# Output-projection weights from the third pair of heads on loaded from GpSimd's own queue, each behind the low part that frees its place

## The chip, the cores and the metric

One core of one Trainium2 chip runs the kernel. The metric is device time in microseconds (us) of one launch. The kernel before took 1513.62 us, the median of three runs (1512.69 to 1514.01). A change is called faster, the same or slower here with a bound of 0.2%, that is 3.0 us.

## What is computed

A gated cross-attention block on x (4 batches, 512 rows, 1024 columns) with a context of 64 rows a batch, then a feed-forward part, all in float32. Cut to what matters:

```python
x = x + tanh(g_xattn) * attention(layernorm(x), ctx, ctx, mask, wq, wk, wv, wo)
x = x + tanh(g_ffn) * ffn(layernorm(x), weight, bias, gate_w, in_scale, out_scale)

# attention: 32 query heads, 8 key heads, 128 wide, rotary positions
attn = softmax(q @ k.T / sqrt(128) + mask)
out  = (attn @ v).reshape(bs, sq, 32 * 128) @ wo          # wo: 4096 x 1024
# ffn: signs of the weight, scales from a softmax routing over 8 experts
out  = ((x * (routing @ in_scale)) @ sign(weight).T) * (routing @ out_scale) + bias
```

## The kernel before, in words

Every large product is made of float32r parts: a matrix is cast to a high part (`hi`), the rest (`raw - hi`) is its low part (`lo`), and three matmuls (hi by hi, lo by hi, hi by lo) stand for one (`three`, lines 51 to 53). ScalarE casts the high parts, GpSimd subtracts for the low parts of the weights.

The program has four stages. **Preparation** (to about 90 us): keys, values, normalised and turned x. **Heads** (90 to 880 us): queries, scores and softmax of 16 pairs of heads; the probabilities go to a scratch tensor in HBM. **Phases** (880 to 1300 us): eight phases, each one batch by one half of the 1024 output columns. A phase runs over the 16 pairs of heads (`HP`): `probs_times(phase, hp)` adds probabilities by (values by output weights) into four PSUM banks. The products of values and output weights, `values_wo(k, h)`, are made once for two batches; k counts 64 pairs of heads over four rounds (`ROUNDS * HP`), and a round is a long phase, with its `values_wo`, and a short one that uses what was kept. In phase 0 `values_wo` runs two pairs ahead of `probs_times`, in the other long phases three. **Feed-forward** (from 1300 us): blocks of 256 rows.

The output weights are what the change touches. `wo_raw` has two places (`WO_BUFS = 2`) of 512 KB, place k % 2. Pair k passes through these steps:

1. `load_wo(k)` (line 695): SyncE waits until the low parts of pair k - 2 are done, and issues one DMA of 512 KB (line 698). Its semaphore is `wo_in[k % 2]`.
2. `split_wo(k, h)` (ScalarE, line 1120): two casts w_hi<-w_raw, each behind the load.
3. `split_low(k, h)` (GpSimd, line 1363): two subtractions w_lo<-w_raw,w_hi, each behind its cast. The second frees the place for pair k + 2.
4. `values_wo(k, h)` (TensorE), then `split_vw` (ScalarE, lines 1128 and 1131) and `values_low` (VectorE, lines 1502 and 1505) take its result out of PSUM; `probs_times` waits for these.

The order of each engine is written out by hand. SyncE issues nearly all transfers in one in-order queue: the loads of output weights, the stores and loads of probabilities (lines 677 and 688), x in and x1 out (lines 728 and 733). At which pair of a phase it comes to which `load_wo` stood in three tables, of which one reads

```python
LONG_WO = {0: 7, 1: 8, 2: 9, 3: 10, 4: 11, 5: 12, 6: 13, 7: 14, 8: 15, 9: 16, 11: 17, 12: 18, 13: 19}
```

(at pair hp of a long phase, `load_wo` of pair 16 * round + value). Probabilities are replaced four pairs behind TensorE (`P_LAG`). ScalarE casts pair hp + 5 at pair hp of a long phase (hp + 3 in phase 0), GpSimd runs through all 64 pairs in order, and does the last steps of the softmax between pairs 3 and 8 (`turned_low`, line 1304, `over_sums`, line 1310). In the heads stage GpSimd's order is that of `step` (line 1312 on).

## Time and profile before

| | |
|---|---|
| median of three runs | 1513.62 us |
| the profiled execution | 1511.08 us, its span 1509.3 us |
| mean granted TensorE clock | 0.994 |
| busy: TensorE, weight loads | 1459.8 us (97%), 1205.7 us (80%) |
| busy: VectorE, ScalarE, GpSimd | 990.7 us (66%), 568.8 us (38%), 718.8 us (48%) |
| DMA queues | SyncE's and ScalarE's only carry the large loads: 213.30 MB in q1, 43.9% of 16 engines' span |
| loads of output weights | 64 of 512 KB, 5.0 us median from issue to landing |

A duration in the profile is that of one instruction; matmuls overlap, so that of a row of them the starts tell the pace. "Idle before" is the time for which an engine stood still ahead of an instruction, and behind the arrow stands what ended that. SPq is SyncE's queue: its rows are the issuing of transfers, not the transfers.

### The profile page before, as it was taken

Reading aid. Unit: us, or ns where it says so; the run is one execution under the profiler, and the core shown is the slowest. Engines: PE = TensorE matmul, PEld = TensorE weight load, DVE = VectorE, ACT = ScalarE, POOL = GpSimd, SP = SyncE. Lnnn points to the kernel's source line nnn. Section 1 sums busy time; section 2 is a strip of 40 time slices with the busy share of each in tenths; the row PEclk is TensorE's granted clock in tenths of the full one; section 3 lists DMA queues with packets and bytes.
Section 4 is the critical chain, followed back from the end, with each engine's and each line's share of the span. In section 5 each row is a group of like instructions: output and inputs, shape, how many; then the busy total and the mean of one; then the engine's idle time right before and its main releaser. Section 6 shows DMA issues by size and latency. Waiting matters only on the chain.

```text
span 1509.3 us, 21232 instructions
## 1 busy us (share of the span) xinstructions
PE 1459.8 (97%) x6800; PEld 1205.7 (80%) x6800; DVE 990.7 (66%) x2117; ACT 568.8 (38%) x927; POOL 718.8 (48%) x594
## 2 busy tenths in 40 slices
PE   6989999999999999999999978999999999999998
PEld 5878888888888888888888856887887887878887
DVE  5837788888888887788888885436346246535653
ACT  5732222222222222222222266438348347124542
POOL 5744455554655546545555465325226235025554
PEclk9999999999999999999999999999999999999999
DMA  7830222122221222122211497889989979742321
GB/s 271 292 116 15 80 82 70 50 68 69 76 69 42 76 69 69 56 76 76 69 61 52 102 310 232 271 271 295 328 300 297 338 271 304 259 168 84 112 75 65
DMA packets 105441, 225.99 MB, mean 150 GB/s; under 512 B 11104, under 2 KB 21856, under 8 KB 105248
## 3 DMA queue, kind: packets, MB, share of 16 engines
q1 hardware_dynamic: 99184, 213.30, 43.9%
q10 hardware_dynamic: 6192, 11.86, 2.1%
q8 instruction: 36, 0.59, 0.2%
q14 instruction: 29, 0.24, 0.1%
HBM read 167.45 MB, written 57.67 MB: 149 GB/s over the span
## 4 chain that ended last, share of the span: by engine, by line
PE 84%; issue 3%; POOL 2%; DMA 2%; SPq 1%; DVE 1%; ACT 1%; POOLq 0%; ACTq 0%; DVEq 0%
PE bank L51 19%; PE bank L53 18%; PE bank L52 18%; PE bank L903 7%; PE bank L904 7%; PE bank L905 7%; PE bank L927 5%; DMA w_raw<-in_wo 1%; POOL last_rows L1358 1%; SPq L688 1%; PE bank L942 1%; POOL feed L1350 0%; POOL w_lo L1363 0%; PE bank L951 0%; PE bank L974 0%
## 5 line engine op out<-in xcount | busy, mean ns | idle before, releaser
L51 PE MATMUL bank<-x_hi,w_hi 128*128 128x512 f32 x1024 | 399.9, 391 | 3.9 <-PEq L66 3.9
L52 PE MATMUL bank<-x_lo,w_hi 128*128 128x512 f32 x1024 | 399.6, 390 | 0.0
L53 PE MATMUL bank<-x_hi,w_lo 128*128 128x512 f32 x1024 | 399.6, 390 | 0.0
L1363 POOL TENSOR_TENSOR w_lo<-w_raw,w_hi 128x512 fp32r<-128x512 f32 x128 | 162.4, 1291 | 235.6 <-ACT w_hi L1120 235.6
L1297 POOL TENSOR_TENSOR q_lo<-rot,q_hi 128x512 fp32r<-128x512 f32 x128 | 164.9, 1294 | 185.6 <-ACT q_hi L1061 185.4
L51 PEld LDWEIGHTS bank<-x_hi,w_hi 128*128 128x128 f32 x1024 | 192.9, 188 | 44.2 <-issue 4.1
L52 PEld LDWEIGHTS bank<-x_lo,w_hi 128*128 128x128 f32 x1024 | 193.0, 188 | 40.1
L53 PEld LDWEIGHTS bank<-x_hi,w_lo 128*128 128x128 f32 x1024 | 192.9, 188 | 40.1
L1061 ACT CAST q_hi<-rot 128x512 fp32r<-128x512 f32 x128 | 79.6, 622 | 344.2 <-DVE rot L1423 290.7
L1502 DVE TENSOR_TENSOR project<-bank,project 64x512 fp32r<-64x512 f32 x128 | 87.4, 683 | 166.7 <-ACT project L1128 164.7
L1304 POOL TENSOR_TENSOR pt_lo<-pt,pt_hi 128x512 fp32r<-128x512 f32 x64 | 82.4, 1288 | 144.4 <-ACT pt_hi L1071 144.3
L1418 DVE TENSOR_TENSOR bank<-bank,cos_q 128x512 f32<-128x512 f32 x64 | 44.8, 699 | 136.5 <-PE bank L53 136.5
L927 PE MATMUL bank<-feed,feed 128*128 128x512 f32 x512 | 130.3, 399 | 0.0
L903 PE MATMUL bank<-project,project 128*128 128x512 f32 x320 | 125.4, 392 | 0.0
L905 PE MATMUL bank<-project,project 128*128 128x512 f32 x320 | 124.7, 390 | 0.0
L904 PE MATMUL bank<-project,project 128*128 128x512 f32 x320 | 124.6, 389 | 0.0
L1128 ACT CAST project<-bank 64x512 fp32r<-64x512 f32 x128 | 74.2, 579 | 113.5 <-PE bank L53 111.1
L927 PEld LDWEIGHTS bank<-feed,feed 128*128 128x128 f32 x512 | 95.1, 190 | 21.8 <-issue 2.9
L1065 ACT ACTIVATE shifted<-shifted 128x512 f32<-128x512 f32 x64 | 40.5, 633 | 166.8 <-DVE shifted L1449 166.8
L1505 DVE TENSOR_TENSOR project<-bank,project 64x512 fp32r<-64x512 f32 x128 | 88.8, 694 | 4.0
L1291 POOL TENSOR_TENSOR w_lo<-w_raw,w_hi 128x1024 fp32r<-128x1024 f32 x30 | 72.2, 2406 | 37.6 <-ACT w_hi L1054 37.6
L1120 ACT CAST w_hi<-w_raw 128x512 fp32r<-128x512 f32 x128 | 73.1, 618 | 40.4 <-DMA w_raw<-in_wo 37.5
(141 smaller groups left out, 2632.3 us busy)
## 6 DMA issues: line engine op xcount, KB each, us to landing
project<-probs_scratch SPq DMA_DIRECT2D x160, 256.0 KB, 6.3
w_raw<-in_wo SPq DMA_DIRECT2D x64, 512.0 KB, 5.0
p_left<-probs_scratch SPq DMA_DIRECT2D x96, 256.0 KB, 6.6
w_raw<-in_wq SPq DMA_DIRECT2D x32, 512.0 KB, 5.2
probs_scratch<-pt_hi SPq DMA_DIRECT2D x64, 256.0 KB, 2.6
probs_scratch<-pt_lo SPq DMA_DIRECT2D x64, 256.0 KB, 3.2
x_in<-in_x SPq DMA_DIRECT2D x16, 512.0 KB, 5.4
last_rows<-in_x SPq DMA_DIRECT2D x8, 1024.0 KB, 9.2
```

Source lines behind the costliest of these rows:

```text
L51: pe.matmul(out, hi, rhs_hi, start=first, stop=False, **kw)
L52: pe.matmul(out, hi, rhs_lo, start=False, stop=False, **kw)
L53: return pe.matmul(out, lo, rhs_hi, start=False, stop=last, **kw)
L903: pe.matmul(acc_ps[t][:], p_hi[hp][:, at], vw, start=hp == 0, stop=False)
L904: pe.matmul(acc_ps[t][:], p_hi[hp][:, at], vw_low, start=False, stop=False)
L905: last = pe.matmul(acc_ps[t][:], p_lo[hp][:, at], vw, start=False, stop=hp == HP - 1)
L927: last = pe.matmul(f_ps[c % 2][:], part[j][k // 4][:, k % 4, t * P:(t + 1) * P], w_sign[k][:, h * HW:(h + 1) * HW], start=(k == 0 and n == ...
L1297: nc.gpsimd.tensor_tensor(q_lo[:, c], rot[:, c], q_hi[:, c].bitcast(F32), ALU.subtract).then_inc(q_lo_ready, 1)
L1304: nc.gpsimd.tensor_tensor(pt_lo[:, i], pt[:], pt_hi[:, i].bitcast(F32), ALU.subtract).then_inc(pt_lo_ready, 1)
L1363: nc.gpsimd.tensor_tensor(wo_lo[:, i, h], wo_raw[:, i, h], wo_hi[:, i, h].bitcast(F32), ALU.subtract).then_inc(wo_lo_ready, 1)
L1502: nc.vector.tensor_tensor(vw_first_lo[k % VW_BUFS][rows_of], vw_bank(k, h)[0:SK, :], vw_first_hi[k % VW_BUFS][rows_of].bitcast(F32), ALU.s ...
L1505: nc.vector.tensor_tensor(vw_kept_lo[hp][rows_of], vw_bank(k, h)[SK:P, :], vw_kept_hi[hp][rows_of].bitcast(F32), ALU.subtract).then_inc(vw ...
```

## The change

`load_wo` loses its wait and stays on SyncE for pairs 0 and 1 alone. The 62 others are issued by GpSimd, by a new function `next_wo(k)` that stands in its program right behind the second low part of pair k, waits until that is complete, and issues the load of pair k + 2 into the same place. These loads have semaphores of their own (`wo_next`), for which ScalarE's casts wait. The three tables and all their calls on SyncE go.

```diff
-    FIRST_WO = {5: 11, 6: 12, 7: 13, 8: 14, 9: 15, 11: 16, 12: 17, 14: 18, 15: 19}
...
+        wo_next = [sem(f"wo_next{i}") for i in range(WO_BUFS)]
...
             def load_wo(k):
 
-                wait(sp, wo_lo_ready, 2 * (k - WO_BUFS) + 2)
                 sp.dma_start(wo_raw[:, k % WO_BUFS], a["wo"][k // HP % NH, k % HP]).then_inc(wo_in[k % WO_BUFS], 16)
...
-            load_wo(2)
-            load_wo(3)
             sp.wait_ge(masked_ready, HEAD_STEPS)
             first_probs(10)
-            load_wo(4)
...
                 for hp in range(HP):
-                    if hp in upcoming and rnd * HP + upcoming[hp] < ROUNDS * HP:
-                        load_wo(rnd * HP + upcoming[hp])
                     due = place(phase, hp) - P_LAG
...
-                act.wait_ge(wo_in[k % WO_BUFS], 16 * (k // WO_BUFS + 1))
+                if k < WO_BUFS:
+                    act.wait_ge(wo_in[k], 16)
+                else:
+                    act.wait_ge(wo_next[k % WO_BUFS], 16 * (k // WO_BUFS))
...
+            def next_wo(k):
+
+                if k + WO_BUFS < ROUNDS * HP:
+                    pool.wait_ge(wo_lo_ready, 2 * k + 2)
+                    nxt = k + WO_BUFS
+                    pool.dma_start(wo_raw[:, k % WO_BUFS], a["wo"][nxt // HP % NH, nxt % HP]).then_inc(wo_next[k % WO_BUFS], 16)
+
             over_key_heads(pool, step)
+            next_wo(0)
             split_low(1, 0)
             query_low(LAST_G, STEPS_G - 1)
             split_low(1, 1)
+            next_wo(1)
             for k in range(2, ROUNDS * HP):
                 for h in range(2):
                     split_low(k, h)
+                next_wo(k)
                 if k == 3:
                     turned_low(LAST_G, 5)
                     over_sums(LAST_G, 6)
```

SyncE's queue before, at the end of the softmax and the beginning of phase 0 (w_raw<-in_wo at L698 are the loads of pairs 9 and 10, then 11, then 12; project and p_left are places of the probabilities; last_rows is the place of x):

```order
L698 DMA w_raw<-in_wo 128x1024 [waits wo_lo_ready] x2
L677 DMA probs_scratch<-pt_hi 128x512 [waits pt_lo_ready,pt_hi_ready]
L677 DMA probs_scratch<-pt_lo 128x512
L780 DMA gate_x<-in_g_xattn 128x1 [waits pt_stored1,pt_stored0]
L781 DMA gate_f<-in_g_ffn 128x1
L728 DMA last_rows<-in_x 128x4x512
L688 DMA project_0_6<-probs_scratch 128x512 [waits av_done]
L688 DMA project_1_6<-probs_scratch 128x512
L698 DMA w_raw<-in_wo 128x1024 [waits wo_lo_ready]
```

The same place of SyncE's queue now:

```order
L675 DMA probs_scratch<-pt_hi 128x512 [waits pt_lo_ready,pt_hi_ready]
L675 DMA probs_scratch<-pt_lo 128x512
L768 DMA gate_x<-in_g_xattn 128x1 [waits pt_stored1,pt_stored0]
L769 DMA gate_f<-in_g_ffn 128x1
L725 DMA last_rows<-in_x 128x4x512
L686 DMA project_0_6<-probs_scratch 128x512 [waits av_done]
L686 DMA project_1_6<-probs_scratch 128x512
```

The load of pair 11 no longer stands behind the wait for the stored probabilities, x and two loads of probabilities. GpSimd before, from the low parts of pairs 4 to 6 on:

```order
L1363 TENSOR_TENSOR w_lo<-w_raw,w_hi 128x512 [waits wo_hi_ready] x6
L1304 TENSOR_TENSOR pt_lo<-pt,pt_hi 128x512 [waits pt_stored0,pt_hi_ready]
L1310 TENSOR_TENSOR probs<-shifted,row_inv 128x512 [waits pt_ready,inv_ready]
L1363 TENSOR_TENSOR w_lo<-w_raw,w_hi 128x512 [waits wo_hi_ready] x4
L1304 TENSOR_TENSOR pt_lo<-pt,pt_hi 128x512 [waits pt_stored1,pt_hi_ready]
L1363 TENSOR_TENSOR w_lo<-w_raw,w_hi 128x512 [waits wo_hi_ready] x48
```

GpSimd now, from the low parts of pair 6 on (L1350 are the low parts, L1357 the loads of pairs 8, 9, 10 and 11):

```order
L1350 TENSOR_TENSOR w_lo<-w_raw,w_hi 128x512 [waits wo_hi_ready] x2
L1357 DMA w_raw<-in_wo 128x1024 [waits wo_lo_ready]
L1291 TENSOR_TENSOR pt_lo<-pt,pt_hi 128x512 [waits pt_stored0,pt_hi_ready]
L1297 TENSOR_TENSOR probs<-shifted,row_inv 128x512 [waits pt_ready,inv_ready]
L1350 TENSOR_TENSOR w_lo<-w_raw,w_hi 128x512 [waits wo_hi_ready] x2
L1357 DMA w_raw<-in_wo 128x1024 [waits wo_lo_ready]
L1350 TENSOR_TENSOR w_lo<-w_raw,w_hi 128x512 [waits wo_hi_ready] x2
L1357 DMA w_raw<-in_wo 128x1024 [waits wo_lo_ready]
L1291 TENSOR_TENSOR pt_lo<-pt,pt_hi 128x512 [waits pt_stored1,pt_hi_ready]
L1350 TENSOR_TENSOR w_lo<-w_raw,w_hi 128x512 [waits wo_hi_ready] x2
L1357 DMA w_raw<-in_wo 128x1024 [waits wo_lo_ready]
```

The issue of a load stands between two pairs of low parts, and ahead of GpSimd's last steps of the softmax.

## Rows read from the trace of the kernel before

**Rows 1.** The page: engines, and TensorE in 40 equal slices of the span

```profile
PE 1459.8 (97%) x6800; PEld 1205.7 (80%) x6800; DVE 990.7 (66%) x2117; ACT 568.8 (38%) x927; POOL 718.8 (48%) x594
PE   6989999999999999999999978999999999999998
```

**Rows 2.** Busy time by stretch: start:end, length, then engines, granted clock, DMA share, GB/s

```profile
878.00:888.00 10.00, 7.48 (x25) 5.14 (x24) 8.27 (x16) 5.22 (x9) 5.44 (x5) 0.83 0.95 330
...
928.00:938.00 10.00, 5.62 (x24) 4.05 (x22) 3.12 (x5) 4.50 (x8) 2.84 (x3) 1.00 0.90 316
938.00:948.00 10.00, 9.87 (x37) 8.04 (x38) 5.50 (x8) 7.01 (x13) 5.48 (x5) 0.83 0.85 276
```

**Rows 3.** TensorE in order of time: start, duration, instruction [idle before <-what ended it]

```profile
887.72 0.47 PE L51 MATMUL bank<-w_hi,project 128*128 128x512 f32 x1 [0.90 <-ACT w_hi L1120]
888.98 0.47 PE L51 MATMUL bank<-w_hi,project 128*128 128x512 f32 x1 [0.33 <-POOL w_lo L1363]
...
928.22 0.39 PE L905 MATMUL bank<-project,project 128*128 128x512 f32 x1
...
932.30 0.39 PE L905 MATMUL bank<-project,project 128*128 128x512 f32 x1
936.70 0.47 PE L51 MATMUL bank<-w_hi,project 128*128 128x512 f32 x1 [4.01 <-DVE project L1505]
...
1265.71 0.47 PE L51 MATMUL bank<-w_hi,vt_left 128*128 128x512 f32 x1 [1.88 <-ACT w_hi L1120]
```

**Rows 4.** The chain that ended last, around the longest of these waits

```profile
919.72 4.06 DMA probs_scratch<-pt_lo
...
924.70 0.43 SPq L728
925.18 0.50 SPq L688
...
926.20 7.15 DMA w_raw<-in_wo
```

**Rows 5.** SyncE's queue in order of time: issues only

```profile
875.52 7.56 SPq L698 DMA_DIRECT2D w_raw<-in_wo  x2
...
1252.92 0.56 SPq L728 DMA_DIRECT2D last_rows<-in_x  x1
1256.01 0.33 SPq L698 DMA_DIRECT2D w_raw<-in_wo  x1
```

**Rows 6.** GpSimd in order of time

```profile
868.06 2.54 POOL L1363 TENSOR_TENSOR w_lo<-w_raw,w_hi 128x512 fp32r<-128x512 f32 x2 [0.17 <-ACT w_hi L1120]
872.34 1.05 POOL L1310 TENSOR_TENSOR probs<-shifted,row_inv 128x512 f32<-128x512 f32 x1
876.21 1.27 POOL L1363 TENSOR_TENSOR w_lo<-w_raw,w_hi 128x512 fp32r<-128x512 f32 x1 [2.82 <-ACT w_hi L1120]
...
912.98 5.03 POOL L1363 TENSOR_TENSOR w_lo<-w_raw,w_hi 128x512 fp32r<-128x512 f32 x4
...
920.85 2.55 POOL L1363 TENSOR_TENSOR w_lo<-w_raw,w_hi 128x512 fp32r<-128x512 f32 x2 [1.59 <-ACT w_hi L1120]
```

**Rows 7.** ScalarE in order of time: casts that waited for a load

```profile
885.65 1.14 ACT L1120 CAST w_hi<-w_raw 128x512 fp32r<-128x512 f32 x2 [3.81 <-DMA w_raw<-in_wo]
...
933.37 1.14 ACT L1120 CAST w_hi<-w_raw 128x512 fp32r<-128x512 f32 x2 [6.07 <-DMA w_raw<-in_wo]
```

**Rows 8.** Line 698: issue to landing, of the 5 loads from 1150 to 1170 us

```profile
DMA to landing us min/median/max: 3.4/4.3/7.3
```

**Rows 9.** GpSimd's shortest instruction, by form: busy us, mean ns of one

```profile
L1381 POOL MEMSET ffn_minus_one<- 128x2 f32 x1 | 0.1, 100 | 0.0
```

**Rows 10.** The page: low parts of the output weights, and of the heads' weights

```profile
L1363 POOL TENSOR_TENSOR w_lo<-w_raw,w_hi 128x512 fp32r<-128x512 f32 x128 | 162.4, 1291 | 235.6 <-ACT w_hi L1120 235.6
...
L1291 POOL TENSOR_TENSOR w_lo<-w_raw,w_hi 128x1024 fp32r<-128x1024 f32 x30 | 72.2, 2406 | 37.6 <-ACT w_hi L1054 37.6
```

**Rows 11.** SyncE's queue: what it waited for from 850 to 1300 us (us, times, longest)

```profile
SPq L698 <- POOL w_lo L1363: 195.3, 57, 8.7
```

More of the change, by code:

```diff
@@ L344, in attend_and_finish @@
     SHORT_VW = {4: 0, 8: 1, 12: 2}
-    FIRST_WO = {5: 11, 6: 12, 7: 13, 8: 14, 9: 15, 11: 16, 12: 17, 14: 18, 15: 19}
-    LONG_WO = {0: 7, 1: 8, 2: 9, 3: 10, 4: 11, 5: 12, 6: 13, 7: 14, 8: 15, 9: 16, 11: 17, 12: 18, 13: 19}
-    SHORT_WO = {4: 20, 8: 21, 12: 22}
     P_LAG = 4
@@ L757, in _ @@
             over_key_heads(sp, step)
-            load_wo(2)
-            load_wo(3)
             sp.wait_ge(masked_ready, HEAD_STEPS)
             first_probs(10)
-            load_wo(4)
             first_probs(11)
-            load_wo(5)
             store_probs(LAST_G, 5)
             first_probs(12)
-            load_wo(6)
             first_probs(13)
-            load_wo(7)
             first_probs(14)
-            load_wo(8)
             store_probs(LAST_G, 6)
             first_probs(15)
-            load_wo(9)
-            load_wo(10)
             store_probs(LAST_G, 7)
@@ L784, in _ @@
             for phase in range(PHASES):
-                rnd, long = phase // PB, phase % PB == 0
-                upcoming = SHORT_WO if not long else FIRST_WO if rnd == 0 else LONG_WO
                 for hp in range(HP):
-                    if hp in upcoming and rnd * HP + upcoming[hp] < ROUNDS * HP:
-                        load_wo(rnd * HP + upcoming[hp])
                     due = place(phase, hp) - P_LAG
```

## The prediction

> **What bounds the kernel now.** I read the page first. TensorE is busy for 97% of the span, and its slices are full but for the beginning and one place, the 24th and 25th slice, with the digits 7 and 8 [rows 1]. A slice is 37.7 us, so that place is 868 to 943 us: the end of the heads and the start of phase 0. Everything that the change touches lies from there to 1300 us. The granted clock and the busy time by stretch come next: of the 10 us from 928 on TensorE works 5.62, and in the 10 us behind that the mean granted clock is 0.83; from 878 on both happen together [rows 2]. In the order of time on TensorE I then looked for idle times and for what ended them. Those that lead back to a load of output weights are few: 0.90 and 0.33 us before pair 2, 4.01 us before the instruction at 936.70, and 1.88 us at 1265.71 in the last long phase [rows 3]. The other waits of the stretch, each 0.3 to 2.1 us, end on the last steps of the softmax, and the change leaves them.
>
> The chain that ended last tells how the 4.01 us came about [rows 4]. SyncE first waits until the last low part of the probabilities is stored (919.72 and 4.06 us), then issues the two gates, x (1 MB) and two loads of probabilities (256 KB each), and only then, at 926.20, the load of pair 11, which takes 7.15 us to land. ScalarE had stood still for 6.07 us by then [rows 7]. The place of this load had been free since 920.85 + 2.55 = 923.40 us, when GpSimd ended the low parts of pair 9 [rows 6]. So 2.8 us are lost before the issue, and more behind it, since the load stands behind 1.5 MB in the same queue: loads that found less ahead of them landed in 3.4 us at best and 4.3 in the median [rows 8].
>
> **Two places make a loop.** Low parts of pair k end, the load of pair k + 2 is issued, lands, its first half is cast (0.6 us, half of the 1.14 in [rows 7]), two low parts take 2.54 us [rows 6], and the place is free again. With the median landing that is 0.6 + 2.54 + 4.3 = 7.4 us for two pairs. TensorE needs 18 matmuls for a pair: 4.08 us from 928.22 to 932.30 [rows 3], 8.2 us for two. The loop has 0.8 us to spare where nothing delays a load.
>
> **What the change takes away.** SyncE spent 195.3 us of its queue in waiting for low parts, in 57 waits [rows 11]. That is no time of TensorE: where SyncE had been waiting before the low part ended, the load was issued at once. The gain is where it came late or had traffic ahead.
>
> *Pair 11.* Pair 9's low parts depend on what GpSimd does between. From 912.98 on it works on pairs 7 and 8 for 5.03 us without a break [rows 6]; two issues now stand in it, so the last low part of the probabilities ends some 2 us later and pair 9's about 0.5 us later, at 923.9. With the issue the load is on its way at 925, about when x is, from another queue. I take 5 us for landing, between 4.3 and 7.15, counted from the start of the issue: 929 us instead of 933.35. TensorE resumed 3.35 us behind the landing (936.70 - 933.35), so now at 932.4 to 933, and it was free at 932.7. Of 4.01 us some 0.6 are left: 3.4 saved. The stretch behind had a clock of 0.83, 1.7 us lost in 10, which I expect back, since the two stretches with such a drop in [rows 2] are the ones in or just behind which TensorE was busy for 7.5 and 5.6 of 10 us. **Together -5.1 us.**
>
> *Pair 2.* The place is free at 868.06 + 2.54 = 870.6 us, SyncE issues at 875.52 [rows 5], behind 20 loads of probabilities, and ScalarE waits 3.81 us, until 885.65 [rows 7]. Now GpSimd issues behind its row at 872.34 [rows 6], at 873.4, in idle time, since it then waited until 876.21 [rows 6]. The load is 2 us earlier and shares the engines with the backlog instead of standing behind it. The 0.90 and 0.33 us [rows 3] should go: **-1.2 us**. The pause ahead of them, and its slow clock, stays.
>
> *The last long phase.* The load issued at 1256.01 stood behind x, issued at 1252.92 [rows 5], and 1.88 us of TensorE followed [rows 3]. From its own queue it should land 1 to 2 us earlier, less a later issue: **-0.9 us**.
>
> **What it adds.** GpSimd issues 62 loads and waits before each until its own low part is complete. No row shows an issue on GpSimd. The bounds are its shortest instruction, 0.10 us, and its longest, 2.41 us [rows 9, 10]. I take 1.05 us, that of the row at 872.34, one pass of GpSimd over 128 partitions and the middle of the range [rows 6]. Nothing speaks for less than none. The same load took SyncE 0.33 us [rows 5], so the loop grows by 0.7 us, to 8.1, against 8.2. With the median it still fits; with a load of 5 us it does not, by 0.6. In the long phases from the second round on ScalarE works two pairs ahead of TensorE (8.2 us), which covers that. In phase 0 the lead is smaller, and of its pairs behind 938 us I charge three turns at 0.3 us: **+1.0 us**. Between 893 and 925 the loop is not what ends the waits. GpSimd's 62 issues in sum, 65 us, fit into the 235.6 us in which it waited for casts [rows 10]. SyncE's queue moves ahead: loads of probabilities go as soon as TensorE has used the old ones, some pairs earlier than before. TensorE waited for none of them before, so that gives nothing; x and x1 go earlier too, but for the first x, 2 us later and not wanted before phase 0 ends. The feed-forward part is as it was.
>
> **Sum**, against the profiled execution of 1511.1 us: -5.1 - 1.2 - 0.9 + 1.0 = -6.2, so 1504.9. Its runs' median lies 2.5 us above that execution: 1507.4 us, 0.4% less.
>
> **A rule against this.** In the rows, the load of pair 11 took 7.15 us and others in a thinner stretch 3.4 to 4.3 [rows 4, 8]; I read the difference as the 1.5 MB ahead of it in the queue. The Trainium skill, DMA: Bandwidth & Descriptors, section "Issuing engines are not separate DMA queues", says that transfers from all engines interleave on the same 16 DMA engines, and that a second issuing engine saves only the time of the issue. The same page, "Queues, rings and completion order", says that each of these engines takes turns between queues, packet by packet; by that a load on its own queue would pass a backlog. No row before shows two loaded queues side by side in this stretch.
>
> **The rivals.**
> 1. *Only the issue moves.* The 7.15 us are the price of the traffic, whichever queue the load is in. Then pair 11 starts at 925 less about 0.3 instead of 926.20 and TensorE's wait shrinks by 1.5 us; a pause of 2.5 remains, the clock may or may not drop. Pair 2 gives 0.5, the last phase nothing, the loop costs 1.0: -1.0 to -2, 1512 us, not to be told from no change. By the first of the two rules of the Trainium skill (DMA: Bandwidth & Descriptors) it would be this one. For it: the DMA engines' share is 0.90 from 928 to 938 us [rows 2]. Against it: loads of the same size landed in half the time. Chance 0.22.
> 2. *GpSimd becomes the bound (slower).* If an issue holds GpSimd, or delays the landing, by x us more than SyncE's did, the loop is 7.4 + x against 8.2. With x = 2.1 (its longest instruction) it lacks 1.3 us for two pairs: 8 turns of phase 0, 10 us; three long phases of 6.5 turns, 8.5 us each less the lead of 8.2, 1 us; and GpSimd's last steps of the softmax come late. +11 to +14 less the 6 of gains: 1520 us. It decides from about 8 (x - 0.8) = 7, x = 1.7. For it: nothing shows the price of an issue. Against: GpSimd waits 235.6 us for casts [rows 10]. Chance 0.15.
> 3. *More than the one load.* All loads from 883 to 925 land nearer 3.4 than 5 us, ScalarE never stands, and half of the small waits of phase 0 go as well, another 3 to 4 us: 1503.5 us. Chance 0.13.
>
> That the loads aren't moved at all is excluded by the order. The forecast has 0.50.
>
> **How the numbers follow.** The forecast's own range is 1504 to 1510, from an issue of 0.10 to 1.3 us and a landing of 4.3 to 6 us. With the third rival and the first it reaches from 1503 to 1513, and part of the second brings it to 1517; what lies outside is the dear half of the second, and a gain beyond the third. Faster by over 0.2% (3.0 us, what a measurement of this kernel can tell from no change): 0.50 + 0.13 = 0.63. Within it: 0.22. Slower: 0.15.
>
> **What would show it.** In the profile after: an issue on GpSimd's queue of about 1 us, 62 times; SyncE's waits for low parts gone; no wait of TensorE over 1.5 us from 889 to 1300 us; ScalarE's wait of 6.07 us at most 2; the clock at 1.00 from 928 to 948; loads of output weights at 4 to 5 us in the median. Issues of more than 1.7 us, or waits of TensorE for casts spread over all long phases, would prove the forecast wrong towards slower. A pause of over 2 us left in front of pair 11's or 12's products with a landing of 7 us would be the first rival.

## The result and the profile after

| kernel | median us | runs | lowest to highest | profiled execution | span |
|---|---|---|---|---|---|
| before | 1513.82 | 4 | 1512.69 to 1514.33 | 1511.08 | 1509.3 |
| after | 1525.45 | 4 | 1523.72 to 1525.68 | 1525.49 | 1523.7 |

The ratio is 1.0075, interval 1.0058 to 1.0093: **slower**, where I had forecast 0.4% less. By the medians the change costs 11.6 us. The profiled execution is 14.4 us longer, because that of before lies 2.7 us below the median of its runs; every table of phases below is read from one profile for each kernel. The page of after, against [rows 1] and [rows 10]:

```profile
span 1523.7 us, 21232 instructions
PE 1464.0 (96%) x6800; PEld 1204.3 (79%) x6800; DVE 990.7 (65%) x2117; ACT 568.2 (37%) x927; POOL 754.4 (50%) x656
PE   5889999999999999999999978999999999999998
L1350 POOL TENSOR_TENSOR w_lo<-w_raw,w_hi 128x512 fp32r<-128x512 f32 x128 | 162.3, 1283 | 194.9 <-ACT w_hi L1107 194.8
w_raw<-in_wo POOLq DMA_DIRECT2D x62, 512.0 KB, 6.1
```

Nothing in the busy times tells where the time went: GpSimd has 62 more instructions and 36 us more, and TensorE is busy for 96%. The one number that speaks is the last: a load of output weights takes 6.1 us in the median to land; on the page of before it took 5.0.

The view that answers is that of the windows, one for each phase. TensorE does the same 272 matmuls in each of the three long phases that follow phase 0. First after, then before; the columns are the length, the busy time of TensorE, of its weight loads, of VectorE, ScalarE and GpSimd, the granted clock, the DMA share and GB/s.

```profile
1012.14:1078.24 66.10, 63.45 (x272) 50.01 (x271) 38.51 (x56) 45.05 (x78) 39.98 (x40) 1.00 0.83 258
1125.85:1191.70 65.85, 63.77 (x272) 51.55 (x271) 38.51 (x57) 46.02 (x79) 39.86 (x38) 0.97 0.83 261
1239.30:1304.60 65.30, 63.69 (x272) 49.91 (x271) 41.45 (x64) 45.16 (x76) 34.18 (x34) 1.00 0.80 249
```

```profile
1008.08:1070.70 62.62, 61.82 (x272) 50.47 (x271) 38.52 (x56) 45.06 (x78) 33.12 (x28) 1.00 0.88 284
1118.30:1180.69 62.39, 61.74 (x272) 50.53 (x271) 38.53 (x56) 46.06 (x79) 33.05 (x26) 1.00 0.88 285
1228.29:1293.18 64.89, 62.26 (x272) 50.38 (x271) 41.45 (x63) 45.17 (x76) 29.02 (x25) 1.00 0.86 287
```

Each window runs from one end of a phase to the next; an end is the start of VectorE's four instructions that add the last products of a phase to x. In the first two long phases all is the same work, 3.5 us longer. In the second of them the clock has a part in it: by its mean of 0.97 it stood for a short time at the lower of its two levels (1.2 GHz instead of 2.4), which takes 1.7 of the 65.85 us, and before has 1.00 there. TensorE's idle time, the length less its busy time, is 2.65 us in the first of them instead of 0.80. GpSimd's busy time grows by 6.9 us, its 12 issues. The DMA share falls from 0.88 to 0.83: the same bytes in a longer time. What changed is when they are carried, and beside what. The 14.4 us, by the same marks:

| part | before | after | difference |
|---|---|---|---|
| until GpSimd's first low part of output weights | 868.06 | 869.23 | +1.2 |
| from there to the end of phase 0 | 92.46 | 95.32 | +2.9 |
| long phases 2, 4, 6 | 62.62, 62.39, 64.89 | 66.10, 65.85, 65.30 | +3.5, +3.5, +0.4 |
| short phases and the feed-forward part | | | +0.1 |
| from the end of GpSimd's last addition to the end of the span | 2.52 | 5.39 | +2.9 |

The first line lies ahead of the change; over all the profiles below that moment lies between 865.4 and 870.3, so it is chance. The last long phase is 64.9 us here and up to 67.9 in other profiles with all loads on SyncE and the same order in that phase (z1_early), so nothing is read from it alone. The same holds for small differences in phase 0: the mean granted clock over it is 0.96 in before and 0.94 in x3_one, whose code is the same up to the last long phase, and that alone is 1.7 us.

**The start of phase 0.** TensorE, then ScalarE and GpSimd, in order of time, beside [rows 3, 7, 6]:

```profile
894.93 0.47 PE L51 MATMUL bank<-w_hi,project 128*128 128x512 f32 x1 [2.18 <-DVE project L1502]
...
927.72 0.47 PE L51 MATMUL bank<-w_hi,project 128*128 128x512 f32 x1 [0.51 <-ACT w_hi L1107]
...
942.04 0.49 PE L51 MATMUL bank<-w_hi,project 128*128 128x512 f32 x1 [2.48 <-POOL w_lo L1350]
```

```profile
930.60 1.14 ACT L1107 CAST w_hi<-w_raw 128x512 fp32r<-128x512 f32 x2 [0.49 <-DMA w_raw<-in_wo]
...
938.72 1.14 ACT L1107 CAST w_hi<-w_raw 128x512 fp32r<-128x512 f32 x2 [4.20 <-DMA w_raw<-in_wo]
```

```profile
893.26 0.57 POOL L1357 DMA_DIRECT2D w_raw<-in_wo  x1 [0.30 <-POOL w_lo L1350]
893.85 1.28 POOL L1291 TENSOR_TENSOR pt_lo<-pt,pt_hi 128x512 fp32r<-128x512 f32 x1
...
926.83 0.57 POOL L1357 DMA_DIRECT2D w_raw<-in_wo  x1 [0.30 <-POOL w_lo L1350]
927.42 2.54 POOL L1350 TENSOR_TENSOR w_lo<-w_raw,w_hi 128x512 fp32r<-128x512 f32 x2
930.25 0.57 POOL L1357 DMA_DIRECT2D w_raw<-in_wo  x1 [0.30 <-POOL w_lo L1350]
```

Pair 11, whose load landed in 3.7 us, is as forecast: ScalarE waits 0.49 us for it, not 6.07. The next one, pair 12, is issued at 930.25 and lands 8.4 us later; ScalarE waits 4.20 us, TensorE 2.48. That load was no quicker before. The load of pair 12 in before, issued at 927.78:

```profile
DMA to landing us min/median/max: 8.5/8.5/8.5
```

TensorE's pause ahead of pair 11 had hidden it. What is new are the loads behind it: those of pairs 13 to 16 took 3.5 to 4.4 us before and take 6.6 to 8.8 now. SyncE's queue tells what lay beside them:

```profile
928.76 0.43 SPq L725 DMA_DIRECT2D last_rows<-in_x  x1
929.24 14.15 SPq L686 DMA_DIRECT2D project<-probs_scratch  x20
```

x and twenty loads of probabilities in 14 us. No low part held SyncE back any more, so the queue let go at once what before had gone out two and four at a time, each time behind a load of weights. The windows, against [rows 2]:

```profile
888.00:898.00 10.00, 6.78 (x28) 4.77 (x27) 7.82 (x17) 7.45 (x14) 7.48 (x8) 1.00 0.85 254
928.00:938.00 10.00, 10.00 (x45) 8.26 (x44) 5.50 (x8) 5.49 (x10) 5.65 (x6) 1.00 0.91 286
938.00:948.00 10.00, 7.42 (x25) 5.26 (x25) 5.51 (x8) 6.91 (x12) 6.15 (x6) 0.83 1.03 384
948.00:958.00 10.00, 9.13 (x39) 6.94 (x39) 5.42 (x8) 7.13 (x14) 6.21 (x6) 1.00 1.05 391
```

The ten microseconds that TensorE had lost are full, and the two windows behind are not: DMA share over 1.0, and again a mean granted clock of 0.83. The 2.18 us at 894.93 are the other new wait. At first it looks like the price of an issue: GpSimd's low part of the probabilities starts at 893.85, directly behind an issue, and before it started at 891.32, or 1.4 us earlier when the 1.2 us ahead of the change are taken off. But x4_act (below), where GpSimd issues nothing, has the same wait:

```profile
894.86 0.77 PE L51 MATMUL bank<-w_hi,project 128*128 128x512 f32 x1 [2.23 <-DVE project L1510]
```

and x2_tiny, where GpSimd issues and the loads stay on SyncE, has 0.77 us there, near the 0.58 of before. So the wait came with the loads' other queue, not with GpSimd's issue. In both kernels that have it ScalarE first stood still for the load of pair 3 (2.68 us in after, 2.57 in x4_act), which landed at 889.7 in after and at 887.0 before (1.2 us of the difference lie ahead of the change).

**A long phase.** SyncE's queue in the first of them, after, and then before:

```profile
1019.88 0.38 SPq L725 DMA_DIRECT2D last_rows<-in_x  x1
1020.31 39.18 SPq L686 DMA_DIRECT2D project<-probs_scratch  x20
```

```profile
1020.50 0.33 SPq L698 DMA_DIRECT2D w_raw<-in_wo  x1
1020.88 0.90 SPq L688 DMA_DIRECT2D p_left<-probs_scratch  x2
...
1028.65 0.33 SPq L698 DMA_DIRECT2D w_raw<-in_wo  x1
1029.03 1.61 SPq L688 DMA_DIRECT2D p_left<-probs_scratch  x2
1030.69 0.59 SPq L728 DMA_DIRECT2D last_rows<-in_x  x1
```

Before, one load of weights went out, and right behind it two of probabilities: the weights had the start on what followed. Now the probabilities go when TensorE frees their places, and x goes 7.7 us into the phase instead of 22.6. From 1012 to 1078 us a load of weights lands in 4.4, 6.0 and 8.0 us (least, median, most); those of before in 3.6, 4.7 and 7.8. The waits of 850 to 1310 us:

```profile
ACT w_hi L1107 <- DMA w_raw<-in_wo: 55.5, 34, 4.4
POOL w_raw L1357 <- POOL w_lo L1350: 18.1, 61, 0.3
```

ScalarE waits for 34 loads and 55.5 us, where before it was 20 and 37.5.

### The profile page after: what moved, and what is told of

It is laid out like the page before. It is cut to its first block, busy times and chain, and to the rows that moved or that the text cites. A ratio compares the mean times of both kernels' runs of the same rounds, so it can differ in the third digit from the quotient of the medians.

```text
span 1523.7 us, 21232 instructions
## 1 busy us (share of the span) xinstructions
PE 1464.0 (96%) x6800; PEld 1204.3 (79%) x6800; DVE 990.7 (65%) x2117; ACT 568.2 (37%) x927; POOL 754.4 (50%) x656
## 4 chain that ended last, share of the span: by engine, by line
PE 82%; POOL 4%; DMA 3%; issue 3%; DVE 1%; ACT 1%; POOLq 0%; ACTq 0%; DVEq 0%; SPq 0%
PE bank L51 19%; PE bank L52 19%; PE bank L53 19%; PE bank L887 7%; PE bank L889 7%; PE bank L888 7%; PE bank L911 5%; DMA w_raw<-in_wo 3%; POOL w_lo L1350 2%; POOL last_rows L1345 1%; PE bank L926 1%; POOL feed L1337 0%; PE bank L935 0%; PE bank L958 0%; PE bank L903 0%
## 5 line engine op out<-in xcount | busy, mean ns | idle before, releaser
L1350 POOL TENSOR_TENSOR w_lo<-w_raw,w_hi 128x512 fp32r<-128x512 f32 x128 | 162.3, 1283 | 194.9 <-ACT w_hi L1107 194.8
L1107 ACT CAST w_hi<-w_raw 128x512 fp32r<-128x512 f32 x128 | 73.2, 618 | 58.2 <-DMA w_raw<-in_wo 55.5
L1502 DVE TENSOR_TENSOR project<-bank,project 64x512 fp32r<-64x512 f32 x128 | 88.8, 694 | 4.0
```

Of the source, the lines that this page charges most:

```text
L1350: nc.gpsimd.tensor_tensor(wo_lo[:, i, h], wo_raw[:, i, h], wo_hi[:, i, h].bitcast(F32), ALU.subtract).then_inc(wo_lo_ready, 1)
L1502: nc.vector.tensor_tensor(vw_kept_lo[hp][rows_of], vw_bank(k, h)[SK:P, :], vw_kept_hi[hp][rows_of].bitcast(F32), ALU.subtract).then_inc(vw ...
```

## The experiments

All ratios are against runs of before on the same chip; the phases are from one profile each, and before's phases are those of the first profile. P0 is the time from GpSimd's first low part of output weights to the end of phase 0, P2, P4 and P6 are the long phases, "tail" is the last line of the table above. "Landing" is the median from issue to landing of the output weights, by the page.

| kernel | ratio [95%] | P0 | P2 | P4 | P6 | tail | landing |
|---|---|---|---|---|---|---|---|
| before | 1 | 92.5 | 62.6 | 62.4 | 64.9 | 2.5 | 5.0 |
| after | 1.0075 [1.0058, 1.0093] | 95.3 | 66.1 | 65.9 | 65.3 | 5.4 | 6.1 |
| x2_tiny | 1.0034 [1.0019, 1.0049] | 94.3 | 63.4 | 64.9 | 65.4 | 5.4 | 4.8 |
| x4_act | 1.0014 [0.9999, 1.0029] | 91.8 | 64.6 | 64.6 | 64.4 | 2.5 | 5.8 |
| x3_one | 1.0028 [1.0015, 1.0041] | 93.0 | 62.8 | 62.5 | 69.0 | 2.5 | 5.0 |
| y1_after_thin | 0.9952 [0.9935, 0.9969] | 89.8 | 61.2 | 61.2 | 61.2 | 5.4 | 3.8 |
| y2_before_thin | 0.9953 [0.9936, 0.9971] | 92.3 | 61.2 | 61.2 | 61.2 | 2.5 | 3.4 |
| x1_paced | 1.0137 [1.0118, 1.0155] | 93.1 | 68.7 | 69.3 | 71.0 | 5.4 | 6.6 |
| u1_landed | 1.0134 [1.0100, 1.0167] | 93.5 | 70.5 | 69.2 | 68.8 | 5.4 | 6.3 |
| v1_behind | 1.0074 [1.0059, 1.0090] | 92.1 | 64.7 | 64.4 | 68.0 | 5.4 | 5.5 |

### What an issue on GpSimd costs: x2_tiny, t8_tiny, t32_tiny

Before, with 62 DMAs that nobody needs (128 rows of 4 bytes) on GpSimd, each where the change has its load and behind the same wait. The other two issue only the first 8 and the first 32.

```
+            def next_tiny(k):
+                if k + WO_BUFS < ROUNDS * HP:
+                    pool.wait_ge(wo_lo_ready, 2 * k + 2)
+                    pool.dma_start(tiny[:, k:k + 1], a["g_xattn"]).then_inc(tiny_in, 16)
```

> The kernel before, and behind each pair of low parts GpSimd also waits and issues a DMA of 128 rows of 4 bytes that nobody needs. Loads of output weights stay on SyncE. Theory 'GpSimd's issue': GpSimd is held 0.9 us a pair, which delays low parts, so +3 to +8 us. Theory 'pacing': under +1.5 us in the phases. Theory 'end': any use of GpSimd's DMA queue adds about 2.9 us behind the last store, which both others have to be read on top of: 1516.7 if the phases cost nothing.

> The kernel before with 8 unneeded DMAs of 128 rows of 4 bytes on GpSimd (62 of them gave 5.4 us from GpSimd's last addition to the end of the span, one load gave 2.48, as in the kernel before). If the end's 2.9 us grow with the number: 2.8 to 2.9 us here. If there is a threshold: 2.5 or 5.4.

> The same with 32. If the end's 2.9 us grow with the number: 3.9 to 4.0 us here. If there is a threshold: 2.5 or 5.4, and with the run above it tells on which side.

An issue keeps GpSimd for 0.56 us, and it waits 0.30 us before it for its own low part. In the profile that goes with 1.9 us more in P0, 0.8, 2.5 and 0.5 in the long phases and 2.9 in the tail: 8.6 us. By the runs it is 0.34%, 5.1 us (2.9 to 7.4), so that 2.3 us (0 to 4.5) are left for the phases instead of 5.7. The windows of P0 and of the second long phase tell why the profile shows more; before, P0 has a mean clock of 0.96 and the long phase 1.00:

```profile
866.47:960.80 94.33, 79.63 (x314) 60.29 (x313) 64.78 (x119) 62.52 (x110) 64.40 (x61) 0.93 0.85 265
1119.40:1184.26 64.86, 63.30 (x272) 51.70 (x271) 38.56 (x57) 46.07 (x79) 40.16 (x39) 0.97 0.89 286
```

The time at 1.2 GHz that these means stand for is worth up to 3.4 us more in P0 and 1.7 in the long phase than before, by the trace's clock; whether the issues brought it is not shown. t32_tiny made 11 issues in the first long phase, where x2_tiny made 13, and it took 62.7 us, as before:

```profile
1010.59:1073.27 62.68, 61.70 (x272) 50.52 (x271) 38.56 (x56) 45.11 (x78) 38.70 (x39) 1.00 0.85 279
```

P0 is longer in all three, 94.1 us with 8 DMAs, 94.8 with 32 and 94.3 with 62, each time with more time at the lower clock than in before. The loads of weights stayed on SyncE and land as before.

**The tail.** It is 2.5 us with 8 DMAs (one run, 1511.51 us), 2.9 with 32 (one run, 1514.62 us), 5.4 with 62. The expectations, growth with the number or a threshold, seem both missed. The trace shows what it is. GpSimd's last instruction but for semaphores is a DRAIN, which starts 1.3 us before its last addition ends. It takes, with 0 (before), 1 (x3_one), 8, 32 and 62 DMAs (after), in nanoseconds, as least, median and most of the one instruction:

```profile
L359 POOLq DRAIN  x1: 1372/1372/1372, 1505.5 to 1505.5; - x1
L359 POOLq DRAIN  x1: 1457/1457/1457, 1507.2 to 1507.2; - x1
L360 POOLq DRAIN  x1: 2038/2038/2038, 1505.9 to 1505.9; - x1
L360 POOLq DRAIN  x1: 3998/3998/3998, 1508.6 to 1508.6; - x1
L356 POOLq DRAIN  x1: 6447/6447/6447, 1517.0 to 1517.0; - x1
```

That is 0.08 us more for every DMA that GpSimd has issued, in proportion, whether of 4-byte rows (x2_tiny has 6448) or of 512 KB. SyncE waits beside it for the last store, until 2.3 us behind the addition, so with 8 DMAs the longer DRAIN is hidden, and with 32 (2.7 us) it begins to show. What the DRAIN does with each of them is not shown.

### Whose queue, and what it shares: x4_act and x3_one

x4_act is the change with the 62 loads issued by ScalarE, each behind the same low part, between its own instructions. x3_one is before with the load of the last pair alone moved to GpSimd.

```
-                    pool.dma_start(wo_raw[:, k % WO_BUFS], ...).then_inc(wo_next[k % WO_BUFS], 16)
+                    act.dma_start(wo_raw[:, k % WO_BUFS], ...).then_inc(wo_next[k % WO_BUFS], 16)
```

> As the change, but the 62 loads are issued by ScalarE behind its copies of the product of the pair before, each behind its low part. A queue of its own for the weights and SyncE freed, but no GpSimd DMA and no software queue. Theory 'pacing': the loads still land in 5.5 to 6.5 us and TensorE still waits in phases 0, 2 and 4: 1518 to 1522. Theory 'GpSimd's issue': with the issue off GpSimd and no cost at the end, 1508 to 1512.

> The kernel before with one load, that of the last pair, issued by GpSimd. Theory 'end' (a fixed cost at the end of a kernel that uses GpSimd's DMA queue at all): +2.5 to +3 us, 1516.5, and 5.4 us instead of 2.5 from the last addition of GpSimd to the end of the span. Its rival, that the 2.9 us at the end come from the 62 loads or by chance: no difference, 1513.8.

With ScalarE as issuer the tail and P0 are those of before or better, but two of the long phases stay 2 us longer, and a load lands in 5.8 us. GpSimd has no DMA in it, so this part comes with the second queue, not with GpSimd. It is not the queue alone: ScalarE now also waits for low parts between its casts. In the profiles the parts nearly add up: x4_act's phases and tail sum to +3.0 us (-0.7, +2.0, +2.2, -0.5), x2_tiny's to 8.6, together 11.6 of the 13.2 us that the change costs from its first line on. By the runs they do so less well: 0.14% and 0.34% are 0.48% of the 0.75%, and the rest is about what the three intervals leave open.

The single load of x3_one, GpSimd's row, SyncE's beside it and TensorE's:

```profile
1273.59 0.73 POOL L1380 DMA_DIRECT2D w_raw<-in_wo  x1 [0.30 <-POOL w_lo L1369]
```

```profile
1270.08 10.79 SPq L689 DMA_DIRECT2D project<-probs_scratch  x14
```

```profile
1284.22 0.61 PE L51 MATMUL bank<-w_hi,vt_left 128*128 128x512 f32 x1 [2.15 <-ACT w_hi L1126]
```

It took 8.6 us to land. The same load on SyncE's queue in before, issued at 1274.09, took 4.0. A wait of 2.15 us of TensorE follows from one load. The 0.28% of the runs, 4.2 us (2.3 to 6.2), is more than that, and so are the 4.1 us of P6. The window from that wait on tells most of the rest:

```profile
1284.00:1294.00 10.00, 9.78 (x36) 7.70 (x37) 5.90 (x11) 6.37 (x9) 2.46 (x5) 0.83 0.63 198
```

Behind the wait a part of it is at 1.2 GHz, another 1.7 us lost, as from 938 on in before. z1_early, which has no DMA on GpSimd, lost 3.0 us in P6 against before, with a wait of 3.6 us instead of 1.9 and a mean clock of 0.97 instead of 1.00. So a long P6 is a late load and what the clock adds, whichever queue the load was in.

### Without the probabilities' traffic: y1_after_thin and y2_before_thin

After and before, each with the reloads of probabilities behind phase 0 cut to 16 of 512 columns. Both leave out most of the probabilities that the later phases read, so their results are wrong and they tell of time alone.

```
-                    sp.dma_start(part[hp].bitcast(F32), scratch["probs"][n, hp, :, batch * S:(batch + 1) * S]).then_inc(p_in[hp], 16)
+                        sp.dma_start(part[hp].bitcast(F32)[:, 0:16], scratch["probs"][n, hp, :, batch * S:batch * S + 16]).then_inc(p_in[hp], 16)
```

> The change, with the loads of probabilities for all phases but the first cut to 16 of 512 columns (the rest is stale, so this leaves out most of the reloaded probabilities); number and order of transfers stay. Theory 'priority' (in SyncE's one queue the weights stood ahead of the probabilities issued behind them; in two queues both share the engines, and a load of weights takes 5.5 to 8 us instead of 4): with nothing to share with, loads of weights land in 3.5 to 4.2 us, phases 2 and 4 fall from 66 to 62 us and under those of the kernel before. Theory 'GpSimd's issue' (0.9 us longer loop, or a slower software queue): loads stay over 5 us, phases 2 and 4 at 65 us. 5.4 us at the end stay with both.

> The kernel before with the same cut loads of probabilities, as the control: it leaves out the same. Both theories: weights land in 3.5 to 4.5 us, phases 2 and 4 at 61.4 to 62.3 us, the wait before pair 11's product in phase 0 about as before or shorter. The difference to the run above, outside of the 2.9 us at the end, is then what GpSimd's issue costs without traffic: 'priority' says under 1 us a long phase, 'GpSimd's issue' 3 us.

The first long phase of y1_after_thin, and the loads by the pages of the two:

```profile
1004.87:1066.07 61.20, 61.20 (x272) 50.67 (x271) 38.56 (x57) 46.15 (x79) 40.64 (x41) 1.00 0.52 162
```

```profile
w_raw<-in_wo POOLq DMA_DIRECT2D x62, 512.0 KB, 3.8
```

```profile
w_raw<-in_wo SPq DMA_DIRECT2D x64, 512.0 KB, 3.4
```

61.20 us is TensorE without a gap, and both kernels reach it in all three long phases, with GpSimd's issues and without. So the issues alone do not make a long phase longer here: they can do it only where a load lands late as well. In P0 y1_after_thin is 2.5 us shorter than y2_before_thin and 5.5 shorter than after: without the traffic the change has a gain there (the pause ahead of pair 11, 4.19 us in y2_before_thin, is gone in it), though y2_before_thin also has more time at the lower clock in P0, which takes up to 3.4 us. The tail takes back 2.9. The two end at the same time, 0.9952 and 0.9953 of before.

### The order of the two queues: x1_paced, u1_landed, v1_behind

The change with SyncE's waits put back where its loads of weights stood, without the loads: until the low parts are done that free the place (x1_paced), until the load has landed (u1_landed), or until GpSimd has issued it, told by a one-column MEMSET behind the issue (v1_behind).

```
+                wait(sp, wo_lo_ready, 2 * (k - WO_BUFS) + 2)
```

```
+                    sp.wait_ge(wo_next[k % WO_BUFS], 16 * (k // WO_BUFS))
```

```
+                    sp.wait_ge(wo_issued, k - WO_BUFS + 1)
```

> The change, with one part undone: SyncE keeps its waits for low parts where its loads of output weights stood, and issues nothing there. GpSimd issues the 62 loads as in the change. Theory 'pacing' (the waits on SyncE spread the loads of probabilities; without them these go in bursts and the weights share the engines with them, 7 to 9 us for a load instead of 4): most of the loss in the phases comes back, loads of weights land in 4.5 to 5 us in the median, time 1514 to 1518. Theory 'GpSimd's issue' (0.3 us of waiting for its own low part and 0.57 us of issue lengthen the loop of two places, and the software queue is slower): the loss stays, 1523 to 1526, landing 6 us.

> The change, but where SyncE's load of output weights stood it now waits until that load, issued by GpSimd, has landed, and only then issues the next loads of probabilities. Theory 'priority': this gives the weights back their place ahead of the probabilities, so they land in 4 to 4.8 us and phases 2 and 4 take 62 to 63.5 us, against 66 in the change and 69 with the waits for low parts. Theory 'GpSimd's issue': the 0.9 us stays in the loop and phases 2 and 4 take 64.5 us or more.

> The change, but SyncE issues its loads of probabilities right behind GpSimd's issue of the load of weights (GpSimd sets one column of a small tensor behind its issue, and SyncE waits for that): the order of issue of the kernel before, in two queues. 'Order of issue counts': weights land in 4 to 4.8 us, phases 2 and 4 take 63 to 64.5 us. 'Two queues share the engines in whatever order, one queue serves the first first': weights land in 5.5 to 6.5 us with the probabilities issued just behind, phases 2 and 4 at 66 to 69 us.

x1_paced missed both of its theories: 1534.5 us, where one gave 1514 to 1518 and the other 1523 to 1526. So it is not the spacing by the waits as such that was lost. In x1_paced the wait that releases SyncE also releases GpSimd, and SyncE is the quicker: the probabilities go out just ahead of the weights each time. The long phases take 69 to 71 us, and from 1012 to 1078 us the loads land in 5.6, 6.9 and 7.8 us; none is quick any more. In v1_behind they go out just behind, and the long phases take 64.7, 64.4 and 68.0 us. Between these two kernels little but the order of issue differs (and a MEMSET of 0.1 us for each load), and it is worth 3.0 to 4.9 us a long phase and 0.6% of the time. Against the change itself v1_behind gains nothing in sum (1.0074 beside 1.0075): 3.3 us less in P0 and 1.4 and 1.5 in P2 and P4, 2.7 more in P6 and 2.2 more in the short phases. That it stays above the 62.5 us of before is partly the price of GpSimd's issues, so how much more an order within one queue is worth cannot be told from it. u1_landed refuted what I had thought: I had expected 62 to 63.5 us from holding the probabilities until the weights are there, and got 69 to 70. My reading is that, held back so long, they meet the next load of weights; it is not tested.

### Repairing the order in one queue: z1_early, z2_late_x, z3_order, z4_x_sooner

If the order is what counts, pair 11's load can be put right without a second queue. All four are before with that load ahead of the wait for the stored probabilities and the first x later in phase 0.

```
             store_probs(LAST_G, 7)
+            load_wo(11)
...
-            load_x(0)
...
+                    if phase == 0 and hp == 8:
+                        load_x(0)
```

z2_late_x moves the later x of the long phases as well, from step 3 to 12. z3_order takes step 8 for them and spreads the loads of phase 0:

```
-    FIRST_WO = {5: 11, 6: 12, 7: 13, 8: 14, 9: 15, 11: 16, 12: 17, 14: 18, 15: 19}
+    FIRST_WO = {5: 12, 6: 13, 7: 14, 8: 15, 9: 16, 11: 17, 13: 18, 15: 19}
...
-                    if phase >= 1 and hp == 3:
+                    if phase >= 1 and hp == (8 if long else 3):
```

z4_x_sooner is z3_order with the first x at step 4.

> The kernel before; on SyncE the load of pair 11 goes ahead of the wait for the stored probabilities, and the first x, which stood ahead of it, goes to pair 8 of phase 0. No GpSimd DMA. My reading of the 4.01 us wait (late issue, and 1.5 MB ahead in the same queue): it goes, with its slow clock, phase 0 shorter by 4 to 5.5 us, time 0.9965 to 0.9975 of before, 1508.5. The rival, that the wait moves to pair 12 or 13: 0.999 to 1.000.

> As z1_early, and in the long phases x is loaded at pair 12 instead of pair 3, behind most loads of weights. Theory 'priority' (what stands ahead of a load of weights in its queue is what delays it): phase 6 falls from 64.9 to 62.5 us, phases 2 and 4 by 0 to 0.5, so another 2 to 3 us less than z1_early. Risk: x comes too late for the end of the phase, then TensorE waits at the start of the next one and a phase grows by some us.

> The kernel before with SyncE's order mended: pair 11 ahead of the wait for the stored probabilities, pairs 12 and 13 one pair of heads earlier, the first x at pair 8 of phase 0, and x in the long phases at pair 8 instead of 12 as in z2_late_x, where it came too late for the end of the phase (67 us). No GpSimd DMA. Theory 'priority': phase 0 shorter by 2 to 4 us, phases 2 and 4 at 62 to 62.5, phase 6 at 63.5: 1507 to 1509, 0.996 to 0.998 of before. If x is still too late, phases 2 and 4 are over 63.

> z3_order with the first x at pair 4 of phase 0 instead of pair 8. If x at pair 8 delays the loads of pairs 15 and 16, which TensorE waited 2.0 us for, phases 0 and 1 together fall from 138.0 to 136.0 to 137.0 us and the time by 1 to 2 us; if x is then ahead of pair 12's load as it was of pair 11's, they take 138.5 to 140 us and the time is 1502.

| kernel | ratio [95%] | median us | P0 | P2 | P4 | P6 |
|---|---|---|---|---|---|---|
| z1_early | 0.9984 [0.9970, 0.9998] | 1509.2 | 91.8 | 62.6 | 62.9 | 67.9 |
| z2_late_x | 1.0052 [1.0033, 1.0070] | 1519.3 | 91.2 | 67.4 | 66.6 | 63.4 |
| z3_order | 0.9924 [0.9904, 0.9943] | 1500.4 | 88.8 | 61.2 | 61.2 | 62.1 |
| z4_x_sooner | 0.9964 [0.9951, 0.9977] | 1506.7 | 89.2 | 61.2 | 61.2 | 61.9 |

z1_early gains little, 0.16% where I had expected 0.25 to 0.35. The load of pair 11, issued ahead of x, lands in 3.3 us instead of 7.15, and its pause is gone, but waits of 1.3 us at pairs 12 and 15 have come: the rival, that the wait moves on, was near. With x at step 12 the first two long phases lose 4 to 5 us: x, issued at 1064.1, took 12.3 us to land, and VectorE waited 12.3 us for it. With x at step 8 they take 61.20 us. The first long phase of z3_order ends 61.20 us behind the phase before:

```profile
1006.87 2.73 DVE L1515 SCALAR_TENSOR_TENSOR last_rows<-bank,tanh_x,last_rows 128x512 f32<-128x512 f32 x4 [6.13 <-PE bank L907]
1068.07 2.73 DVE L1515 SCALAR_TENSOR_TENSOR last_rows<-bank,tanh_x,last_rows 128x512 f32<-128x512 f32 x4 [3.44 <-PE bank L907]
```

It is 0.76% faster than before, with all traffic in place, by the order of the same transfers in one queue. Its loads of weights land in 4.7 us in the median, hardly sooner than the 5.0 of before: what decides is which of them are late, and the median does not tell that. In P0 it gains 3.6 us, of which the next phase loses 1.6 again (49.2 us); the 4.01 us of [rows 3] were to be had there. z4_x_sooner has the same long phases, 136.7 us for phases 0 and 1 together, as its expectation has it, and a profile with a span of 1496.5 us, the shortest of all. Yet that is its fastest run; the runs lie between 1498.3 and 1508.6. Why its median is higher than that of z3_order stays open.

## Why the prediction was wrong

**The step that failed** is the last of "What it adds": "SyncE's queue moves ahead: loads of probabilities go as soon as TensorE has used the old ones, some pairs earlier than before. TensorE waited for none of them before, so that gives nothing". Nothing waited for them, and they still cost. Each of SyncE's 57 waits for low parts [rows 11], which I took for idle time of a queue, ended with a load of weights, and the loads of probabilities, 256 KB each, stood behind it. With both gone, the same bytes run ahead of the weights and beside them. y1_after_thin shows it from one side (without them 61.2 us for a long phase instead of 66.1), x1_paced and v1_behind from the other (69 and 64.5 us, by the order of issue). The waits alone, put back without the loads, did not help; it was the order that they kept. The first two long phases, which the forecast had at nothing, lost 7.0 us.

The same mistake is in "shares the engines with the backlog instead of standing behind it": the load of x3_one that shared them took 8.6 us, where it had taken 4.0 in SyncE's queue. The Trainium skill, DMA: Bandwidth & Descriptors, says in "Queues, rings and completion order" that each DMA engine takes turns between the queues that have work for it; the 8.6 us agree with that. In the prediction I read that rule as one in favour of the change. It is in favour only of what is short beside a long backlog, and the weights were mostly the ones ahead.

*Pair 11, -5.1.* Its own wait went, as worked out (4.01 to 0.51 us). The pause moved to pair 12 at 2.48 us and the clock of 0.83 stayed, in the same ten microseconds. From 928 to 958 TensorE works 26.55 us instead of 25.49 (5.62 + 9.87 [rows 2] and 10.00 in the third window): **-1.1 us instead of -5.1** by that rough measure. I had asked what is late next for GpSimd, and not which load is: pair 12's load had taken 8.5 us before as well, 3.0 us behind pair 11's landing, and it took 8.4 now. z1_early, which mends pair 11 without a second queue, had the same end: 0.7 us less in P0.

*Pair 2, -1.2.* Its 0.90 and 0.33 us became one of 0.52; then came the 2.18 us at 894.93. The gain was there, 0.7 us, and this wait took back more: it is 1.6 us longer than the 0.58 us at the same place before. It is not GpSimd's issue, since x4_act has it too; ScalarE stood still for the load of pair 3 just before.

*The last long phase, -0.9.* The wait of 1.88 us went; the longest left is 0.31, and TensorE's idle time fell from 2.6 to 1.6 us. But its busy time is 1.4 us longer for the same 272 matmuls, at a granted clock of 1.00 in both, so that the phase takes 0.4 us more. The loads land in 5.8 us in the median there, in both kernels. **Nothing instead of -0.9**; what makes the busy time longer stays open.

*GpSimd's issues, +1.0.* The time of one was about right, 0.57 + 0.30 us where I took 1.05. The sum was too small, by how much is not sure: x2_tiny has **+5.7 us** in phase 0 and the three long ones in its profile, most of it at the lower clock, and **+2.3** (0 to 4.5) by its runs. My loop had 4.3 us for a landing. With the 6.0 us of the first long phase it is 0.3 + 6.0 + 0.6 + 2.54 = 9.4 us for two pairs of 8.2. By that a long phase would lose about 8 us (6.5 turns); it lost 3.5, so the loop gives the direction and not the size. That the issue costs nothing where loads land in 3.8 us, as y1_after_thin has it, is the same loop: 7.2.

*The tail, +2.9.* I had no term for it, and no row of before could have shown it: GpSimd's last DRAIN grows by 0.08 us for each DMA it has issued.

**The rivals.** The first one had the right doubt, that the queue does not shorten a landing, and the wrong size, since it let everything else stand. Its sign came true: a pause over 2 us (2.48) ahead of pair 12's product, with a landing of over 7 us (8.4). The second, given 0.15, gave 1520 us and comes nearest. It asked that an issue hold GpSimd, or delay the landing, by 1.7 us more than SyncE's did; the holding is 0.5 us more (0.87 against 0.33) and the landing 1.3 (6.0 against 4.7 in the first long phase), 1.8 together. What it did not have is why landings grow, nor the place: it put 10 us into phase 0 and 1 us into the long phases, and it was 2.9 and 7.4, with 2.9 at the end.

**What is shown and what is not.** Shown: the time an issue takes on GpSimd, that the loss in the long phases comes without GpSimd as well, that without the traffic there is none, that the order of issue counts, and that the tail is GpSimd's DRAIN. Argued only: that the wait at 894.93 comes from pair 3's load. Not sure in size: what the issues cost in the phases, and how the loss divides between them and the second queue. Open: when the clock falls and when not, which adds 1.7 us each time, and why the first x at step 4 and 8 differ.

## What to carry to other kernels

A wait of a DMA queue can hold the order of what is queued behind it, as here: before a wait that costs nobody anything is removed, list what is queued behind it, and what those transfers will then run beside. In this kernel the order of issue within one queue worked as a priority (pair 11's load, 7.15 us behind x and 3.3 ahead of it), and the second queue gave that up; where one load is late, first try to put it further ahead in the same queue (here 0.76% faster, against 0.75% slower). Transfers that nobody waited for still made those slower that somebody did (landings of 6.1 us with them, of 3.8 without, in the change). And look for the pause that the one you remove was hiding: pair 12's load was as late before.

## What the runs showed of the hardware that I had not expected

- The end of the program took 2.5 us behind the last addition with 0, 1 or 8 DMAs issued by GpSimd, 2.9 with 32 and 5.4 with 62. Issued by ScalarE, 62 left it at 2.5. It is GpSimd's last DRAIN, 0.08 us longer for each DMA that GpSimd issued. GpSimd's last row of work, after and before:

```profile
1517.05 1.26 POOL L1345 TENSOR_TENSOR last_rows<-feed,feed 128x512 f32<-128x512 f32 x1 [2.56 <-DVE feed L1569]
```

```profile
1505.52 1.26 POOL L1358 TENSOR_TENSOR last_rows<-feed,feed 128x512 f32<-128x512 f32 x1 [2.56 <-DVE feed L1572]
```

- GpSimd's issue took 0.57 us, its first in a program 0.73 to 0.74, and nearly every one (61 of 62) waited 0.30 us for the end of the low part ahead of it. For the same load SyncE's took 0.33 us at least and 0.46 in the median (before), ScalarE's 0.34 in the median (x4_act).
- With little else under way a load of 512 KB landed in 3.8 us in the median from GpSimd's queue (y1_after_thin) and 3.4 from SyncE's (y2_before_thin): the queues differ little by themselves.
- The mean granted clock of the same code differs between profiles: 0.96 over phase 0 in before and 0.94 in x3_one, each 0.02 being 1.7 us.
